# Two cross attentions: row sums from one rounded sum of the weights, moved between the scores of the two sequences

## What is computed

```python
# first attention
q = emb @ Wq + bq;  k = latent @ Wk + bk;  v = latent @ Wv + bv
w = softmax((q @ k.T) * scale, axis=rows)
x = w @ v + emb
x = (x - mean(x)) * rsqrt(var(x) + EPS) * gamma + beta
# second attention
Q = x @ Wq + bq;  K = ctx @ Wk + bk;  V = ctx @ Wv + bv
out = x + (softmax((Q @ K.T) * scale, axis=context) @ V) @ Wo + bo
```

## Time and profile before

| | before |
|---|---|
| median of 3 runs | 684.35 us (683.64 to 684.7) |
| the profiled execution | 682.88 us, span 680.8 us |
| granted TensorE clock, mean | 0.997 of 2.4 GHz |
| PE busy | 667.1 us (98%) |
| DVE, ACT, POOL busy | 520.4 (76%), 424.6 (62%), 490.3 us (72%) |
| HBM | 78 GB/s over the span |

### The profile page before, as it was taken

The page is one execution under the profiler, slowest core; times in us unless marked ns, Lnnn a source line. Parts: engine busy times, 40 slices in busy tenths (PEclk is TensorE's granted clock), DMA queues, the critical chain, the costliest instruction groups (busy, mean ns, idle before and its releaser), DMA issues.

```text
span 680.8 us, 12411 instructions
## 1 busy us (share of the span) xinstructions
PE 667.1 (98%) x4047; PEld 589.4 (87%) x4047; DVE 520.4 (76%) x1227; ACT 424.6 (62%) x1037; POOL 490.3 (72%) x394
## 2 busy tenths in 40 slices
PE   8988999999999999999999999999999999999987
PEld 6975888989898898889889888988989898898976
DVE  4889687877868787786878778796877779687765
ACT  2765666576666747666575766656566665666542
POOL 0566968769596877959687795968778695866762
PEclk9998999999999999999999999999999999999999
DMA  9902005050220505032050503104040401302003
GB/s 296 317 6 77 32 2 171 1 170 0 73 96 0 169 0 170 0 94 76 0 169 0 170 0 121 48 10 159 0 170 0 142 28 40 129 0 78 1 1 124
DMA packets 34657, 53.47 MB, mean 79 GB/s; under 512 B 4560, under 2 KB 12752, under 8 KB 34640
## 3 DMA queue, kind: packets, MB, share of 16 engines
q1 hardware_dynamic: 34640, 53.26, 23.7%
HBM read 36.44 MB, written 16.81 MB: 78 GB/s over the span
## 4 chain that ended last, share of the span: by engine, by line
PE 89%; DVE 5%; POOL 2%; ACT 1%; DMA 1%; issue 1%; SPq 0%; DVEq 0%; POOLq 0%
PE bank L418 77%; PE bank L425 12%; DVE n L898 1%; DMA bk_b<-in_L_xattn_bk_dram 1%; POOL n L1215 1%; DVE stats L1054 1%; POOL wq_sb L1221 1%; DVE x_even L1049 0%; DVE rb L981 0%; DVE xT_lo L874 0%; DVE n L1065 0%; POOL rstd L1227 0%; ACT bank L747 0%; ACT n L715 0%; SPq L322 0%
## 5 line engine op out<-in xcount | busy, mean ns | idle before, releaser
L1234 POOL TENSOR_TENSOR prod<-n,u_b 128x512 f32<-128x512 f32 x64 | 81.5, 1297 | 44.7 <-DVE n L1065 39.3
L872 DVE SCALAR_TENSOR_TENSOR y_lo<-bank,terms,y_hi 128x512 fp32r<-128x512 f32 x64 | 48.0, 749 | 62.8 <-ACT y_hi L665 62.8
L1273 POOL TENSOR_TENSOR r<-r,beta_b 128x512 f32<-128x512 f32 x60 | 76.0, 1298 | 0.0
L1266 POOL TENSOR_TENSOR r<-n,gamma_b 128x512 f32<-128x512 f32 x60 | 75.7, 1299 | 0.0
L665 ACT ACTIVATE y_hi<-bank,terms 128x512 fp32r<-128x512 f32 x64 | 43.9, 686 | 39.9 <-PE bank L418 39.9
L1227 POOL TENSOR_TENSOR rstd<-var_eps,minus_half 128x2 f32<-128x2 f32 x32 | 22.4, 699 | 63.5 <-DVE var_eps L1061 63.4
L667 ACT ACTIVATE pc_hi<-bank 128x512 fp32r<-128x512 f32 x32 | 19.2, 598 | 68.2 <-PE bank L418 68.2
L1038 DVE SCALAR_TENSOR_TENSOR r<-bank,rinv,r 128x512 f32<-128x512 f32 x60 | 44.8, 747 | 11.2 <-PE bank L418 11.2
L418 PE MATMUL bank<-wv_hi,wc_hi 128*128 128x512 f32 x128 | 51.6, 403 | 1.8 <-issue 1.8
L747 ACT ACTIVATE bank<-e,neg 128x256 f32<-128x256 f32 x64 | 29.9, 468 | 35.1 <-DVE neg L1000 35.1
L418 PE MATMUL bank<-xT_hi,wqk_hi 128*128 128x512 f32 x128 | 51.2, 400 | 0.0
(11 more groups left out here) (201 smaller groups left out, 2355.0 us busy)
## 6 DMA issues: line engine op xcount, KB each, us to landing
out_dram<-r SPq DMA_DIRECT2D x15, 1024.0 KB, 5.4
x_even<-in_x_dram SPq DMA_DIRECT2D x8, 1024.0 KB, 7.2
ctxn<-in_ctx_dram SPq DMA_DIRECT2D x16, 512.0 KB, 3.7
x_odd<-in_x_dram SPq DMA_DIRECT2D x8, 1024.0 KB, 7.0
rb<-r_rows SPq DMA_DIRECT2D x15, 256.0 KB, 3.8
wq_sb<-in_L_xattn_Wq_dram SPq DMA_DIRECT2D x4, 256.0 KB, 3.4
wk_sb<-in_L_xattn_Wk_dram SPq DMA_DIRECT2D x2, 512.0 KB, 6.8
wv_sb<-in_L_xattn_Wv_dram SPq DMA_DIRECT2D x2, 512.0 KB, 9.2
```

The source lines that it names most:

```text
L872: i = dve.scalar_tensor_tensor(dst, src, bias, high.bitcast(F32), ALU.add, ALU.subtract)
L1234: pool.tensor_tensor(prod[j % 2][:], N[:, j, :], u_b[1][:], ALU.mult).then_inc(prod_ready, 1)
L1266: pool.tensor_tensor(r[:, j, :], N[:, j, :], gamma_b[:], ALU.mult).then_inc(scaled_ready, 1)
L1273: pool.tensor_tensor(r[:, j, :], r[:, j, :], beta_b[:], ALU.add).then_inc(resid_ready, 1)
```

## The change

TensorE's row sums take two products with ones instead of three. GpSimd adds the two high blocks, the two low blocks, and both sums together (into `rb`); ScalarE rounds that full sum to a high part, VectorE subtracts for the low part, and TensorE multiplies both by ones. The row sums now stand behind the scores of the first of the two sequences (`scores1(it, 0)`), and the second sequence is weighed before. On ScalarE the rounding stands between the two roundings of `wc`, and all four bias rows behind them. On VectorE the subtraction and both cuts of `wc` stand ahead of the reading of the row sums. On GpSimd two of the four additions of beta go behind the bias adds. The bank of the row sums becomes bank 7 instead of 5.

```diff
-          + tiles("y1", 2) + [("wc", 0), ("rs", 0), ("wc", 1)] + tiles("s1", 2) + tiles("pr", 2) + tiles("pt", 2)
+          + tiles("y1", 2) + tiles("wc", 2) + [("s1", 0), ("rs", 0), ("s1", 1)] + tiles("pr", 2) + tiles("pt", 2)
...
-        w_lo_sum = Y[1][:, 0, :]
+        w_sum_hi, w_sum_lo = Y[1][:, 0, :], Y[1][:, 1, :]
...
             def row_sums(it):
 
-                pe.wait_ge(w_lo_added, it.times(1, 1))
+                pe.wait_ge(w_sum_cut, it.times(2, 2))
                 dst = begin(it, "rs")
-                end(product(dst[:], [(ones_r[:], W[0][:, :, mt, :]) for mt in range(RM)] + [(ones_r[:], w_lo_sum)]),
-                    "rs")
+                end(product(dst[:], [(ones_r[:], w_sum_hi), (ones_r[:], w_sum_lo)]), "rs")
...
                 if it.front:
                     weigh0(it, 0)
+                    weigh0(it, 1)
+                if it.back:
+                    scores1(it, 0)
+                if it.front:
                     row_sums(it)
-                    weigh0(it, 1)
-                if it.back:
-                    scores1(it)
+                if it.back:
+                    scores1(it, 1)
...
+            def round_w_sum(it):
+                act.wait_ge(w_sums, it.times(3, 3))
+                act.activation(w_sum_hi, RB[:], ACT.Copy).then_inc(w_sum_cut, 1)
...
                 if it.front and not begin_it:
-                    for b in range(2):
-                        round_bank(it, "wc", b, halves(WC[0], b))
-                        bias_of_rows(it, b)
-                    for j in range(2, J):
+                    round_bank(it, "wc", 0, halves(WC[0], 0))
+                    round_w_sum(it)
+                    round_bank(it, "wc", 1, halves(WC[0], 1))
+                    for j in range(J):
                         bias_of_rows(it, j)
...
                 if it.front:
-
+                    dve.wait_ge(w_sum_cut, it.times(2, 1))
+                    dve.tensor_tensor(w_sum_lo, RB[:], w_sum_hi.bitcast(F32), ALU.subtract).then_inc(w_sum_cut, 1)
+                    for b in range(2):
+                        low(it, "wc", b, halves(WC[1], b), halves(WC[0], b), per=2)
                     wait_filled(dve, it, "rs")
...
-                    for b in range(1 if begin_it else 0, 2):
-                        low(it, "wc", b, halves(WC[1], b), halves(WC[0], b), per=2)
...
             def add_w_lo(it):
 
+                def sum_of(dst, w):
+                    pool.tensor_tensor(dst.rearrange("p (b t) -> p b t", b=2), w[:, :, 0, :].bitcast(F32),
+                                       w[:, :, 1, :].bitcast(F32), ALU.add).then_inc(w_sums, 1)
+
+                pool.wait_ge(hi["w"], it.times(2 * RM, 2 * RM))
+                sum_of(RB[:], W[0])
                 wait_emptied(pool, it, "s0", 1)
-                pool.tensor_tensor(w_lo_sum.rearrange("p (b t) -> p b t", b=2), W[1][:, :, 0, :].bitcast(F32),
-                                   W[1][:, :, 1, :].bitcast(F32), ALU.add).then_inc(w_lo_added, 1)
+                sum_of(bias2[:], W[1])
+                pool.wait_ge(w_sums, it.times(3, 2))
+                pool.tensor_tensor(RB[:], RB[:], bias2[:], ALU.add).then_inc(w_sums, 1)
...
                 if it.back:
-                    add_beta(it, range(J))
+                    add_beta(it, (0, 1))
                 if it.front:
                     add_bias(it)
+                if it.back:
+                    add_beta(it, (2, 3))
+                if it.front:
                     rstd_of(it, 0)
```

More of the change, by code:

```diff
@@ L263, in two_cross_attentions @@
         hi = {n: sem(f"{n}_hi_ready") for n in ("xT", "cT", "cn", "y", "w", "wc", "nT", "y1", "pt", "pc")}
-        cn_lo, w_lo_added = sem("cn_lo_ready"), sem("w_lo_added")
+        cn_lo, w_sums, w_sum_cut = sem("cn_lo_ready"), sem("w_sums"), sem("w_sum_cut")
         r0_written, rb_loaded = sem("r0_rows_written"), sem("rb_loaded")
@@ L546, in scores0, with scores1 @@
                     end(mm, "s0", b)
-            def scores1(it):
+            def scores1(it, b):
                 ct = CT[1 - it.parity]
-                for c in range(KC):
-                    wait_emptied(pe, it, "y1", c)
-                for b in range(2):
+                if b == 0:
+                    for c in range(KC):
+                        wait_emptied(pe, it, "y1", c)
+                for b in (b,):
                     dst = begin(it, "s1", b)
@@ L627, in iteration @@
                     weigh0(it, 0)
-                    row_sums(it)
                     weigh0(it, 1)
                 if it.back:
-                    scores1(it)
+                    scores1(it, 0)
+                if it.front:
+                    row_sums(it)
+                if it.back:
+                    scores1(it, 1)
                 if it.last:
@@ L1162, in iteration @@
                     add_betaq(it)
-                    low(it, "wc", 0, halves(WC[1], 0), halves(WC[0], 0), per=2)
                 if it.back:
```

## The result

| | before | after |
|---|---|---|
| median | 684.0 us (682.89 to 684.7, 4 runs) | 712.26 us (711.9 to 712.51, 4 runs) |
| ratio | | 1.0414, 95% interval 1.0396 to 1.0432 |
| the profiled execution | 682.88 us, span 680.8 | 712.43 us, span 710.6 |
| granted TensorE clock, mean | 0.997 | 0.993 |
| PE busy | 667.1 us (98%) | 676.0 us (95%) |

The kernel is 4.1% slower. A steady pair is read from the starts of PE's transposes of x: before, 299.73 and 614.39 are eight pairs apart, after, 313.19 and 600.18 seven.

The account below looks back on a forecast made before the run. PE, with 89% of the chain, was taken to bound the kernel. Fifteen pairs at 1.73 us (26.0) plus 2 for the first pair made 28.0 on 682.88, 710.9; against the median 684.35, 712.4; range 702 to 722 us.

Parts of the forecast that it names:

- The margin at the transposes: ScalarE's exponentials of sequence 0 end 1.87 us before PE transposes them; the change was said to spend this.
- A pair 1.73 longer: Each steady pair: 0.23 us saved on PE against waits of 0.47, 0.97 and 0.51; 26.0 us over 15 pairs.
- The three waits: PE waits 0.47 us before the row sums, then 0.97 and 0.51 for the two sequences' exponentials at the transposes.
- The sum's chain: GpSimd's adds, ScalarE's rounding (0.60 taken), VectorE's subtraction held until 0.55 after GpSimd's operation, costing 0.45 us more.
- Additions of beta behind the bias adds cost nothing: On GpSimd, two additions moved ahead of the reciprocal root cost nothing; without cover the root comes up to 2.5 us later.
- The floor, +0.91 a pair: Even with both sum parts ready when PE arrives, product 2 starts 0.91 us later; 13.6 in 15 pairs, about 698.
- The first pair, 2, between 0 and 3.9: Extra adds, rounding and subtraction delay the first pair's row sums; bounds 0 and 3.9 us, 2 taken.
- The clock stays up: TensorE's granted clock stays near 1, the new waits being shorter than 1.80 us; falling clock, about 742, chance 0.03.
- the chances named: Forecast 0.73, no VectorE hold 0.13, late subtraction 0.05, falling clock 0.03, faster 0.04, same 0.02; some 0.17 outside the range.

Follow-up runs that it names:

- act_order: The changed kernel with two of four bias rows moved behind the exponentials on ScalarE and GpSimd's later additions of beta moved to where it waits; 694.25 us.
- hold_off: The changed kernel, but GpSimd starts its first two additions of beta only when both parts of the sum are there; 705.0 us.
- place_only: The changed kernel with the earlier row sums (three products, one GpSimd add, no rounding or subtraction) in the new place and order; 701.45 us.
- best: combo with the first pair as before the change and VectorE's cut of wc of the second sequence moved behind the row maxima; 684.87 us.
- combo: act_order, with GpSimd's first additions of beta also waiting for both parts of the sum; 687.86 us.
- sum_only: The kernel before with the full sum in two parts and two products, but the row sums left in their old place; 754.1 us.

## Why the prediction was right

The forecast was 712.4 us, slower with 0.94; 712.26 was measured. By its steps, after against prediction:

- *The margin at the transposes is what the change spends.* Right: PE waits for exponentials 31 times, and with two bias rows behind them (act_order) the waits are gone and 1.25 us a pair with them.
- *A pair 1.73 longer.* Measured 1.67. The three waits were put at 0.47, 0.97 and 0.51 and read at 0.33, 0.79 and 0.58; the two matmuls of the sums took 0.56 from start to next start, where 0.46 was reckoned. These make 1.57; most pairs are 40.94 long, 1.61 more than before, and a few of up to 41.20 raise the mean.
- *The sum's chain.* GpSimd's three adds took 3.87 from 330.23 to the next operation at 334.10 (with the wake), reckoned 3.9; the rounding 0.64, inside 0.60 to 0.71. The subtraction ended 0.58 behind GpSimd's addition, reckoned 0.55. The rule of the Trainium skill, "SBUF — State Buffer", section "SBUF: two separate sides", that the loser blocks for the whole instruction, agrees with the 1.10 us here against the 0.69 of hold_off, and GpSimd paid too: its two additions took 2.99 where two took 2.54 before.
- *Additions of beta behind the bias adds cost nothing.* Right: they end as the root's input arrives, and the root starts without a wait at 346.45.
- *The floor, +0.91 a pair.* place_only has no wait for the sums and lies at +1.11 with its third product (0.23) still in; less that, +0.88.
- *The first pair, 2, between 0 and 3.9.* It was 2.85 by the two traces (63.08 to 65.93), of which 0.24 lie ahead of PE's first transposes of x (16.99 and 17.23). The term was a little small: not only the chain, but the GpSimd adds also held VectorE's set-up products (one more of them took 1.77 us instead of 0.68), and PE waited 4.6 us there, after which the granted clock was 0.50 at 47 to 49 us.
- *The clock stays up.* Right in the steady pairs, with a mean of 1.00 over a whole one. The reason given for it was weak: the window of 43 to 45 us lies inside the wait of 1.80 us and not behind it (the trace does have 1.00 there too, over 45 to 51 us), and that shorter waits keep the clock up is not borne out as a rule (last section). The end was left out: in the last pair PE's wait of 2.02 us was followed by a granted clock of 0.59 over 680 to 684 us, and sixteen transposes took 3.06 us where they had taken 1.97. From the start of these transposes to the end the trace after has 30.6 us and before 29.0: 1.6 by the clock.

So in the profile the sum reads 2.85 + 15 x 1.67 + 1.6 = 29.5, against 29.8 us by which the spans differ; the prediction had 28.0. Part of the closeness is luck: the pairs came out 1 us under and the two ends 2.5 over, and the medians differ by 28.3 us where the two profiled executions differ by 29.55. One slip changes nothing: the chances named leave 0.14 outside the range, not 0.17.

```profile
680.00:684.00 4.00, 4.00 (x19) 3.81 (x20) 2.96 (x5) 2.71 (x5) 2.51 (x2) 0.59 0.00 0
```

This window of the changed kernel has the columns of the earlier trace rows.

## What to carry to other kernels

A matmul taken from the engine that bounds the kernel is worth its start-to-start time only while everything behind it keeps its margin: before moving work, find the next thing that engine waits for, and count in the in-order queues what stands between the moved result and that thing. Here 0.23 us were saved and the 1.87 us of margin at the transposes were spent, because the row sums came later and ScalarE, as before, made all four bias rows ahead of the exponentials, which TensorE needed next; two of the four could wait (act_order). Spare time on GpSimd is not free either: in two places an addition held the VectorE operation beside it (1.10 us instead of 0.69, 1.22 instead of 0.54). And look at the first and the last round of a pipeline separately: what is covered in the middle is paid in full there.

## What was not expected of the hardware

The same wait at the end did not always lower TensorE's clock. PE waited for the last pair's rows 2.02 us in the changed kernel and 2.81 in best, and the sixteen transposes behind took 3.06 and 3.54 us; it waited 2.01 in place_only and 2.78 in combo, and they took 1.97. The same holds inside sum_only, where waits of 3.10 and 3.12 us left the clock at 1.00 in two pairs and waits of 3.08 to 3.14 us were followed by 0.50 in the other eleven steady pairs. The length of the wait alone does not decide between the two levels in these runs, and a wait of 2 us can cost 1.6 us of slow matmuls behind it.
